# Two layer normalisations computed with centring and averaging matrices in chunks of 512 tokens, in a deformable-convolution and attention kernel

## What is computed

```python
def _ln_t(v, eps=1e-05):                  # over the 64 channels of a token
    m = jnp.mean(v, axis=-1, keepdims=True)
    s = jnp.var(v, axis=-1, keepdims=True)
    return (v - m) / jnp.sqrt(s + eps)

t = t + attention(_ln_t(t))               # 8 heads, each token sees itself and 31 before it
t = t + experts(_ln_t(t))                 # 32 experts, each takes its 8 best tokens of an image
```

## Time and profile before

| | |
|---|---|
| median of 3 runs | 759.24 us |
| runs | 752.0, 759.24, 760.38 us |
| the profiled execution | 755.67 us |
| its span, first to last instruction | 753.8 us |
| mean granted PE clock | 0.867 |
| last write of the convolution to the start of attention on PE | 409.26 to 436.91 us |
| last product of attention to the first top-8 step of the experts | 679.13 to 703.27 us |

### The profile page before, as it was taken

How to read it: one execution, slowest core, us unless ns; L and a number is a source line. 1 busy time by engine, 2 the same in 40 slices (tenths; PEclk the granted TensorE clock), 3 DMA queues, 4 the chain that set the end, 5 groups by cost and what they waited for, 6 DMA issues and landing times.

```text
span 753.8 us, 32560 instructions
## 1 busy us (share of the span) xinstructions
PE 637.5 (85%) x14954; PEld 474.7 (63%) x14954; DVE 466.5 (62%) x560; ACT 369.4 (49%) x568; POOL 292.9 (39%) x287
## 2 busy tenths in 40 slices
PE   6479998898894898988887687999999999984475
PEld 1156666666742576766666576888888888863253
DVE  0587867788516876777763514766666676648523
ACT  0264555566423655556542433656655665553520
POOL 4045555566301654545540323344344434322200
PEclk9856899999996588999988555999999999997758
DMA  8310000000004000000001710000000000000002
GB/s 300 79 27 3 5 3 5 4 4 4 5 6 92 3 4 3 4 4 5 4 4 30 176 52 1 2 1 0 0 0 0 0 0 0 0 2 0 1 2 116
DMA packets 6403, 18.01 MB, mean 24 GB/s; under 512 B 1869, under 2 KB 4237, under 8 KB 5573
## 3 DMA queue, kind: packets, MB, share of 16 engines
q1 hardware_dynamic: 6286, 16.24, 7.8%
HBM read 12.37 MB, written 3.87 MB: 22 GB/s over the span
## 4 chain that ended last, share of the span: by engine, by line
PE 75%; DVE 7%; ACT 6%; DMA 4%; issue 4%; POOL 1%; SPq 1%; DVEq 0%; ACTq 0%
PE banks L268 21%; PE banks L199 11%; PE banks L844 9%; PE banks L821 5%; PE banks L888 5%; PE banks L869 5%; PE banks L903 4%; PE banks L171 3%; PE banks L185 2%; DMA off<-in_places_dram 2%; ACT y L301 2%; PE banks L834 1%; DMA off<-offsets_dram 1%; PE banks L229 1%; PE banks L615 1%
## 5 line engine op out<-in xcount | busy, mean ns | idle before, releaser
L322 POOL TENSOR_TENSOR y<-hy,hx 128x576 f32<-128x576 f32 (+1 forms) x104 | 167.5, 1633 | 200.4 <-DVE hy L396 197.3
L268 PE MATMUL banks<-y,xt 32*64 32x144 f32 (+1 forms) x6656 | 167.8, 306 | 25.0 <-issue 14.0
L268 PEld LDWEIGHTS banks<-y,xt 32*64 32x64 f32 x6656 | 114.7, 145 | 56.1 <-issue 36.8
L322 DVE TENSOR_TENSOR y<-hy,hx 128x576 f32<-128x576 f32 (+1 forms) x104 | 121.8, 1215 | 5.0 <-DVE hy L396 0.5
L1085 POOL TENSOR_TENSOR y<-y,stats 128x1024 f32<-128x1024 f32 x32 | 60.9, 1902 | 109.1 <-DVE stats L1017 109.0
L349 ACT ACTIVATE hx<-banks 128x768 f32<-128x768 f32 x96 | 62.1, 652 | 61.4 <-PE banks L171 58.6
L354 ACT ACTIVATE hy<-banks 128x768 f32<-128x768 f32 (+1 forms) x92 | 71.8, 805 | 38.5 <-PE banks L185 38.0
L301 DVE COPY y<-banks 128x768 f32<-128x768 f32 x48 | 45.8, 955 | 68.0 <-PE banks L268 68.0
L199 PE MATMUL banks<-y,w_dc 64*64 64x128 f32 x2304 | 84.7, 301 | 2.5 <-issue 1.2
L1007 DVE TENSOR_REDUCE stats<-banks 128x16 f32<-128x1024 f32 x32 | 39.2, 1225 | 69.3 <-PE banks L844 69.3
L199 PEld LDWEIGHTS banks<-y,w_dc 64*64 64x64 f32 x2304 | 75.4, 151 | 9.4 <-issue 7.1
(11 more groups left out here) (141 smaller groups left out, 820.0 us busy)
## 6 DMA issues: line engine op xcount, KB each, us to landing
src<-in_x_dram SPq DMA_DIRECT2D x4, 578.0 KB, 5.6
y<-in_w_dram SPq DMA_DIRECT2D x1, 2080.0 KB
xt<-in_xt_dram SPq DMA_DIRECT2D x1, 2048.0 KB, 11.4
off<-in_w_dram SPq DMA_DIRECT2D x2, 1024.0 KB
out_dram<-tokens SPq DMA_DIRECT2D x4, 512.0 KB, 3.8
offsets_dram<-tokens SPq DMA_DIRECT2D x32, 54.0 KB
off<-offsets_dram SPq DMA_DIRECT2D x16, 108.0 KB
w_dc<-in_w_dc_dram SPq DMA_DIRECT2D x2, 288.0 KB, 9.2
```

The source lines that it names most:

```text
L268: last = nc.tensor.matmul(ap(out, [[UNIT_ROWS * PITCH - 2, 3], [PITCH, strip.n], [1, WIN_COLS]]), m.xt[32 * j:32 * j + 32, strip.tile_row, ...
L322: multiply(dst, hy, hx, ALU.mult).then_inc(cv.s_ready[g], 1)
```

## The change

Both normalisations keep the channels on partitions. A constant `m.centring` holds two 128 x 128 matrices: identity less averaging, and averaging, each block diagonal over the two images' 64 channels. The work goes by 8 chunks of 512 tokens, one PSUM bank each. Per chunk PE makes one product that centres the tokens (banks 0 to 3, in turn) and one that averages the squares (banks 4 and 5), which leaves the variance repeated on all 64 partitions of its image. ACT squares 128 x 512 from PSUM and takes the root of 128 x 512. DVE inverts 128 x 512 and multiplies 128 x 512 from PSUM into `xh`. POOL has no part. The function `norm_pool` and the statistics tiles go.

```diff
 def norm_pe(nc, pe, m, ln, beside):
...
+    def centre(n):
+        pr, half = ln.chunks[n]
+        ln.tokens_ready_pe(pe, n)
+        if n >= 4:
+            pe.wait_ge(ln.normed, n - 3)
+        nc.tensor.matmul(m.ps[:, n % 4, :], m.centring[:, 0, :], m.tokens[:, pr, half * CHUNK:(half + 1) * CHUNK],
+                         start=True, stop=True).then_inc(ln.centred, 1)
+    def average(n):
+        if n in beside:
+            beside[n]()
+        if n == 0:
+            ln.banks_free_pe(pe)
+        if n >= 2:
+            pe.wait_ge(ln.std_ready, n - 1)
+        pe.wait_ge(ln.squared, n + 1)
+        nc.tensor.matmul(m.ps[:, AVERAGES + n % 2, :], m.centring[:, 1, :], ln.square[:, n % 2, :],
+                         start=True, stop=True).then_inc(ln.averaged, 1)
+    centre(0)
+    centre(1)
+    for n in range(NORM_CHUNKS):
+        if n + 2 < NORM_CHUNKS:
+            centre(n + 2)
+        average(n)
 def norm_act(nc, act, m, ln, beside):
...
+    square(0)
+    square(1)
+    for n in range(NORM_CHUNKS):
+        if n in beside:
+            beside[n]()
+        act.wait_ge(ln.averaged, n + 1)
+        if n >= 2:
+            act.wait_ge(ln.normed, n - 1)
+        nc.scalar.activation(ln.rstd[:, n % 2, :], m.ps[:, AVERAGES + n % 2, :], ACT.Sqrt, bias=m.eps_ln[:, 0:1]
+                             ).then_inc(ln.std_ready, 1)
+        if n + 2 < NORM_CHUNKS:
+            square(n + 2)
 def norm_dve(nc, dve, m, ln):
...
+    def invert(n):
+        dve.wait_ge(ln.std_ready, n + 1)
+        nc.vector.reciprocal(ln.rstd[:, n % 2, :], ln.rstd[:, n % 2, :]).then_inc(ln.rstd_ready, 1)
+    invert(0)
+    for n in range(NORM_CHUNKS):
+        pr, half = ln.chunks[n]
+        if n + 1 < NORM_CHUNKS:
+            invert(n + 1)
+        dve.wait_ge(ln.rstd_ready, n + 1)
+        nc.vector.tensor_tensor(ln.xh[pr][:, half * CHUNK:(half + 1) * CHUNK], m.ps[:, n % 4, :], ln.rstd[:, n % 2, :],
+                                ALU.mult).then_inc(ln.normed, 1)
```

```diff
+    def turn(pr):
+        for b in range(PIX // P):
+            if b % 4 == 0 and 2 * pr + b // 4 >= 2:
+                pe.wait_ge(ex.turned_copied, 2 * pr + b // 4 - 1)
+            last = nc.tensor.transpose(m.ps[:, TURNED + b // 4, b % 4 * P:(b % 4 + 1) * P],
+                                       ex.ln.xh[pr][:, b * P:(b + 1) * P], m.identity[:, :])
+            if b % 4 == 3:
+                last.then_inc(ex.turned, 1)
...
+    norm_pe(nc, pe, m, ex.ln, {NORM_CHUNKS - 1: lambda: logits(0)})
     logits(1)
+    for pr in range(PAIRS):
+        turn(pr)
...
+    norm_act(nc, act, m, ex.ln, {})
+    logits(0)
     exponentials(0)
     logits(1)
+    turned(0)
+    turned(1)
     exponentials(1)
+    turned(2)
+    turned(3)
```

More of the change, by code:

```diff
@@ L694 @@
     pass
+CHUNK = PIX // 2
+NORM_CHUNKS = 2 * PAIRS
+AVERAGES = 4
 def norm_pe(nc, pe, m, ln, beside):
[L699 to L719, removed]
-def norm_act(nc, act, m, ln, beside):
[L723 to L727, removed]
+    def centre(n):
[5 more added lines that the diff above has]
+                         start=True, stop=True).then_inc(ln.centred, 1)
@@ L729, in norm_act, with square @@
+def norm_act(nc, act, m, ln, beside):
+    def square(n):
+        act.wait_ge(ln.centred, n + 1)
+        if n >= 2:
+            act.wait_ge(ln.averaged, n - 1)
+        nc.scalar.activation(ln.square[:, n % 2, :], m.ps[:, n % 4, :], ACT.Square).then_inc(ln.squared, 1)
     square(0)
     square(1)
[L731 to L746, removed]
@@ L749, in norm_dve @@
-def norm_dve(nc, dve, m, ln):
[L750 to L783, removed]
@@ L1110, in logits @@
     def logits(group):
-        pe.wait_ge(ex.ln.normed, 2 * group + 2)
-        pe.wait_ge(ex.ln.centred, 3 + group)
+        pe.wait_ge(ex.ln.normed, 4 * group + 4)
         for half in range(2):
             for pr in (2 * group, 2 * group + 1):
-                last = nc.tensor.matmul(m.ps[2 * EXPERTS * (pr % 2):2 * EXPERTS * (pr % 2 + 1), 4 * group + half, :],
+                last = nc.tensor.matmul(m.ps[2 * EXPERTS * (pr % 2):2 * EXPERTS * (pr % 2 + 1), LOGITS[group] + half, :],
                                         m.w_gate[:, :], ex.ln.xh[pr][:, half * BANK:(half + 1) * BANK],
@@ L1127, in experts_pe @@
             for c in range(4):
[L1128 removed]
+                last = nc.tensor.transpose(m.ps[:, PICKS_TURNED[g] + q, c * P:(c + 1) * P],
                                            ex.pick[:, g, (4 * q + c) * P:(4 * q + c + 1) * P], m.identity[:, :])
             last.then_inc(ex.pt_in_psum, 1)
[L1132 removed]
+    pe.wait_ge(ex.turned_copied, 2 * PAIRS)
     pe.wait_ge(ex.pt_ready, 2 * GROUPS)
@@ L1204, in logits @@
         for half in range(2):
-            nc.scalar.activation(ex.pick[:, g, half * BANK:(half + 1) * BANK], m.ps[:, 4 * g + half, :],
+            nc.scalar.activation(ex.pick[:, g, half * BANK:(half + 1) * BANK], m.ps[:, LOGITS[g] + half, :],
                                  ACT.Identity, bias=m.b_gate[:, 0:1]).then_inc(ex.logits_ready, 1)
@@ L1211, in exponentials, with turned @@
                              accum_out=ex.gate_sum[:, g:g + 1]).then_inc(ex.gate_exp, 1)
-    norm_act(nc, act, m, ex.ln, {PAIRS: lambda: logits(0)})
+    def turned(pr):
+        for q in range(2):
+            act.wait_ge(ex.turned, 2 * pr + q + 1)
+            nc.scalar.copy(ex.xt[:, 4 * q:4 * q + 4, pr, :], m.ps[:, TURNED + q, :].rearrange("p (c n) -> p c n", c=4)
+                           ).then_inc(ex.turned_copied, 1)
+    norm_act(nc, act, m, ex.ln, {})
+    logits(0)
     exponentials(0)
     logits(1)
+    turned(0)
+    turned(1)
     exponentials(1)
+    turned(2)
+    turned(3)
     for g in range(GROUPS):
@@ L1295, in program @@
         m.identity = sb("identity", [P, P])
+        m.centring = sb("centring", [P, 2, P])
         m.xt = sb("xt", [P, TR, TC, P])
@@ L1432, in program @@
-        for ln in (at.ln, ex.ln):
-            ln.mean, ln.squares, ln.rstd = (norm_stats[:, k, :, :] for k in range(3))
-            ln.square = s_all[:, 1024:3072].rearrange("p (s b n) -> p s b n", s=2, n=P)
-        for name, ln in (("at", at.ln), ("ex", ex.ln)):
[L1436 to L1445, removed]
+        at.ln.chunks = [(pr, half) for half in range(2) for pr in range(PAIRS)]
@@ L1446, in program @@
+        ex.ln.chunks = [(pr, half) for pr in range(PAIRS) for half in range(2)]
+        for name, ln in (("at", at.ln), ("ex", ex.ln)):
+            ln.square = s_all[:, 1024:2048].rearrange("p (s n) -> p s n", s=2)
+            ln.rstd = s_all[:, 2048:3072].rearrange("p (s n) -> p s n", s=2)
             ln.centred = sem(name + "_centred")
             ln.squared = sem(name + "_squared")
-            ln.squares_summed = sem(name + "_squares_summed")
+            ln.averaged = sem(name + "_averaged")
@@ L1449, in program, with first_tokens, first_banks, second_tokens @@
             ln.std_ready = sem(name + "_std_ready")
             ln.rstd_ready = sem(name + "_rstd_ready")
-            ln.scaled = sem(name + "_scaled")
-            ln.back_in_psum = sem(name + "_back_in_psum")
             ln.normed = sem(name + "_normed")
+        def first_tokens(pe, n):
+            if n == 0:
+                pe.wait_ge(convs[1].finished, FINALS)
+        def first_banks(pe):
+            pe.wait_ge(convs[1].finished, FINALS)
+        def second_tokens(pe, n):
+            pe.wait_ge(at.added, 2 + BLOCKS * (n // 2 + 1))
@@ L1499, in program @@
         ex.gate_rsum = sb("gate_rsum", [P, GROUPS])
+        ex.turned, ex.turned_copied = sem("ex_turned"), sem("ex_turned_copied")
         ex.logits_in_psum = sem("ex_logits_in_psum")
@@ L1537, in program @@
             conv1_loads.append((off_buffer.bitcast(U16)[32 * rg + ROW_COORD:32 * rg + ROW_ONE + 1, :], a["places"][rg]))
-        loads = [(m.identity[:, :], a["identity"]),
+        loads = [(m.identity[:, :], a["identity"]), (m.centring[:, :, :], a["centring"]),
                  (convs[1].w_off[:, :, :], a["w_off2"]), (convs[1].w_dc[:, :, :], a["w_dc2"]),
@@ L1742, in transformer_pe @@
             def transformer_pe():
-                pe.wait_ge(convs[1].finished, FINALS - 1)
-                norm_pe(nc, pe, m, at.ln, {("turn", 2): head_products, ("back", 0): lambda: pe.wait_ge(heads_ready, 2)})
-                pe.wait_ge(at.ln.normed, PAIRS)
+                norm_pe(nc, pe, m, at.ln, {5: head_products})
+                pe.wait_ge(heads_ready, 2)
+                pe.wait_ge(at.ln.normed, NORM_CHUNKS)
                 attention_pe(nc, pe, m, at)
@@ L1797, in constants @@
     c["identity"] = np.eye(P, dtype=f32)
+    average = np.kron(np.eye(P // C), np.full((C, C), 1.0 / C))
+    c["centring"] = np.stack([np.eye(P) - average, average], 1).astype(f32)
     c["spread_q"] = np.tile(np.eye(TQ) * MASK_SCALE, (P // TQ, P // TQ)).astype(f16)
```

26 lines of the change are left out of this document (12 added, 14 removed).

## The result

The changed kernel takes 813.66 us (median of 4 runs, 810.08 to 822.58); the kernel before took 757.38 (4 runs, 752.0 to 760.38). The ratio is 1.074, with a 95% interval of 1.063 to 1.084: slower. (Ratios and intervals leave out executions more than 1.5% above the fastest of the same kernel; medians and stage times do not.) The forecast was 816 us, in a range of 796 to 834. The profiled execution is the slowest of the four, 822.58 us with a span of 820.8, and stands about 9 us over the median; its convolutions alone, which the change does not touch, took 6.4 us more than those of the profile before.

A forecast was written before the change was run, and what follows sets the result against it. The prediction took the chain of waits through both normalisations as the bound, wholly on the path. From 755.7 us by the profiled execution, +30.0 for the first and +30.4 for the second gave 816 us, range 796 to 834.

The forecast's parts named there:

- the ring: Chunks 2 to 5 of each normalisation: multiply, two products, root and reciprocal wait in a closed loop, 8.35 us each.
- The reciprocal: DVE's inversion of 512 columns per chunk, 16 in all: 3.3 us each, from a line through 16 and 64 columns.
- The rival with eight repeats of an ordinary column: DVE's reciprocal at the page's rate, 8.3 ns a column, 4.27 us each; 831.5 us in all, chance 0.12.
- the cheap long row: Rival: DVE's reciprocal costs mostly set-up, 1.0 us for 512 columns; 753 us in all, chance 0.03.
- the short steps: Chunks 6 and 7 of each normalisation, with no centring ahead and the average ready early: 4.65 us each.
- the start: Beginning of a normalisation: four warm products, a root, two reciprocals, a multiply and gaps, 11.7 us.
- The clock in the loops: PE at half speed in all four closed loops per normalisation; the full-clock rival gave 801.5 us, chance 0.14.
- The first normalisation: Convolution's last write to attention's first product: 55.1 us plus 2.5 for head products, 57.6 against 27.65, +30.0 us.
- The second: Normalisation from attention's last product to the first top 8: 55.3 us against 24.14, +31.2, or +30.4 with the table-load saving.
- the saving of the table load: After the second normalisation, the exponential's table load starts while ACT is idle, not behind a copy: 0.8 us back.
- The rows for pooling: 32 new PE turns and 8 ACT copies under DVE's picks: 0 to 2 us lost, taken as 0.
- A warm start: Rival: dense products leave PE at 2.4 GHz when attention begins, -11 us, 805 us in all; chance 0.08.

The follow-up runs named there:

- e2: Changed kernel with PE issuing the average of chunk n ahead of the centring of chunk n + 2; 778.5 us.
- e3: Changed kernel with three buffers for the deviation instead of two, PE's order kept; 813.3 us.
- e4: Changed kernel with both edits, the average ahead of the centring and three deviation buffers; 773.8 us.
- e9_keep_clock: Changed kernel with three more unread products on PE behind each average of chunks 0 to 4; 800.5 us.
- e8_lnexp_order: Changed kernel with root and reciprocal replaced by logarithm and exponential on ACT, and the average issued ahead of the centring; 734.9 us.

## Why the prediction was right, point by point

The mechanism came out as forecast, the ring above all. That the sum came within 2.3 us of the time is in part luck, as the last points show.

**The reciprocal** was put at 3.3 us from rows of 16 and 64 columns; it measured 3.35. The straight line held for eight times the width. The rival with eight repeats of an ordinary column, 4.27 us, falls, and so does the cheap long row. The 16 reciprocals took 53.4 us of DVE, where I wrote 53.

**The ring** was put at 8.35 us and measured 8.49; the short steps at 4.65 measured 4.71; the start, four products to the first multiply, at 11.7 and it ended at 427.35, 11.7 us after 415.65. e2, e3 and e4 took the two waits apart as argued. Within the ring the parts were off both ways: the products took 3.80 us instead of 3.65, the root 0.69 instead of 0.6, the reciprocal 3.35 instead of 3.3, and the multiply 0.56 instead of 0.7. Together these make about the 0.14 us by which the ring was over.

**The clock in the loops** was half, as forecast from the pulses before. The rows of the first normalisation's four loops and of attention's beginning, after:

```profile
427.40:458.10 30.70, 16.57 (x62) 7.15 (x62) 11.69 (x6) 3.52 (x6) 3.79 (x12) 0.56 0.00 0
475.00:489.00 14.00, 13.35 (x100) 10.95 (x102) 3.25 (x5) 3.93 (x7) 0.00 (x0) 0.50 0.11 41
```

The 0.56 is a mean. From 435.9 to 444.4 it was 0.70, yet the two products took 2.08 and 1.72 us there as in the other turns: the clock was up only while PE had nothing to do. In the second normalisation's loops it was 0.62, with products of 2.05 and 1.72 us.

**The first normalisation** was forecast at 57.6 us and measured 59.3. Four rings and two short steps are 0.7 of the difference. Another 0.7 is the head products: from 454.95 to 458.18 they took their full 3.2 us at a clock of 0.50, where I had hoped for a rising clock and taken 2.5. The last 0.3 is the average behind them, 2.02 us instead of 1.72. That the clock rose in the kernel before "at 414 to 419", as I wrote, puts the rise too early: there too it was 0.50 through the head products and the turns behind them (414.3 to 419), and 1.00 from 420 to 423, when PE was busy for 0.6 of 3 us. **The second** was forecast at 55.3 and measured 55.9. Together +63.4 us where I had 30.0 + 31.2, 2.2 too few; the saving of the table load was put at 0.8 and measured 0.75.

**The end** is where a term was wrong, in "The rows for pooling". I took 0, in 0 to 2 us of loss, and looked at the turns only as work to be hidden. They were hidden: the steps between the four top 8 took no longer than before. The end gained 6.4 us in the profile beyond the table load, with the clock at 1.00 in pooling and the first layer. I had named the clock for the normalisations and forgotten it for the stage behind. The stages' sum, 63.4 - 7.2 = 56.2 us, is what the medians differ by, 56.3, where my sum said 60.3. So two misses of opposite sign, 2.2 us too few and 6.4 too many, partly cancelled. The start of the sum, 755.7 us by the profile, lay 1.7 below the median of 757.4 and brought the time nearer still. Runs of one kernel spread by 8 to 12 us, so none of this could be read from the time alone.

**The marks on the time axis**, attention's first product near 467 and the first top 8 near 764, stood at 475.0 and 777.4. Of these 8 and 13.4 us the convolutions made 6.4 and attention 4.3, both of this one execution.

**Attention** was forecast unchanged, and in the experiments' profiles it is: 242.2 to 243.3 us, apart from 246.5 in the changed kernel's own profiled execution.

## What to carry to other kernels

A statistic that a product spreads over all partitions saves the turns, but every later step on it is paid at full width; ask which operation has a price per column above the ordinary, and look for a second form of it in the trace to get its slope. When a loop over chunks is written out by hand, follow each engine's order for an instruction that waits ahead of one that is needed now: here an average behind a centring was worth 35 us of 813. And read the granted clock of each stage, before and after, also behind the change: the same products took 11.7 us at a mean clock of 0.65 and 7.3 at 1.00.

## What the runs showed that I had not expected

Idle work can pay: three unread products behind each of five averages made e9_keep_clock 11 to 13 us faster than the changed kernel. For the 32 unread turns in the kernel before, no gain of the whole is shown.

A warm start did not help attention. I had priced it at 11 us. In e8_lnexp_order PE came out of the normalisation at the full clock, and attention's first product found it so. By 434 the clock was down, and the mean of the next 28 us was 0.53, although PE was busy for 23 of them:

```profile
413.00:432.00 19.00, 16.50 (x80) 7.50 (x80) 5.49 (x9) 16.29 (x28) 4.09 (x16) 1.00 0.42 98
432.00:460.00 28.00, 23.00 (x180) 19.34 (x182) 12.40 (x18) 7.90 (x13) 4.16 (x5) 0.53 0.37 106
```

Attention took 242.4 us there, as ever. So a warm start was not worth the 11 us that I had priced it at, since the clock did not last. Why the clock falls there was not tried.
